# Router logits summed from the old rows' transposed form and eight more columns beside Wo; prefixes among the small moves

## What is computed

```python
x = x + 0.5 * ffn(layernorm(x), ...)
x = x + attn(layernorm(x), ...)        # 16 heads of 8, windows of 64, out @ Wo.T + bo
x = x + 0.5 * ffn(layernorm(x), ...)

# in ffn
r_in = x * rsqrt(mean(x * x) + 1e-6) * rsqrt(d) * router_scale
logits = r_in @ router_w                # 8 experts
top_k_idx = top_k(logits, 2)
out = sum over the two: weight * per_expert_scale * expert(x)
```

## Time and profile before

| | us |
|---|---|
| median of 3 runs | 640.43 |
| lowest, highest | 637.59, 641.42 |
| the profiled execution, device time | 640.15 |
| its span in the trace | 638.1 |
| TensorE busy in the span | 520.2 |
| VectorE, GpSimd, ACT busy | 416.4, 363.3, 277.3 |

### The profile page before, as it was taken

One profiled execution on the slowest core, in us unless ns is written; L12 is line 12 of the kernel. 1 busy time (PEld: TensorE's weight loads), 2 busy tenths in 40 slices (PEclk: granted clock), 3 DMA queues, 4 the chain that ended last, 5 costly groups with the idle time before them and its releaser, 6 DMA issues.

```text
span 638.1 us, 20679 instructions
## 1 busy us (share of the span) xinstructions
PE 520.2 (82%) x7242; PEld 457.1 (72%) x7243; DVE 416.4 (65%) x1431; ACT 277.3 (43%) x627; POOL 363.3 (57%) x425
## 2 busy tenths in 40 slices
PE   0899865999999599999999899999730999999920
PEld 0666635899999478888788778878520999999920
DVE  5776653666676857677688887656324566766747
ACT  0444112443443246666566657555420344434404
POOL 8777775775566431343657565561667556656630
PEclk9999896999999679999899999999855899999975
DMA  9611222222322312010212111120102222323259
GB/s 268 206 48 54 68 70 51 84 71 83 83 82 75 100 51 66 23 52 20 76 30 76 35 40 33 44 55 19 34 27 77 72 81 85 83 74 92 83 143 277
DMA packets 60136, 49.37 MB, mean 77 GB/s; under 512 B 8736, under 2 KB 53536, under 8 KB 59936
## 3 DMA queue, kind: packets, MB, share of 16 engines
q1 hardware_dynamic: 51872, 31.51, 18.6%
q0 software_dynamic: 8192, 16.86, 8.0%
HBM read 23.55 MB, written 20.59 MB: 69 GB/s over the span
## 4 chain that ended last, share of the span: by engine, by line
PE 57%; DVE 13%; POOL 10%; issue 8%; DMA 5%; ACT 3%; SPq 3%; DVEq 0%; POOLq 0%; ACTq 0%
PE PS L560 16%; PE PS L574 7%; PE PS L634 7%; POOL xs_rows L408 6%; PE PS L628 5%; DVE MB L1278 4%; DVE X L1250 4%; PE PS L526 3%; PE PS L549 3%; PE PS L782 2%; POOL ys_rows L423 2%; PE PS L818 2%; DMA XS<-xs_rows 2%; PE PS L624 2%; DMA ys_rows<-YO,XS 1%
## 5 line engine op out<-in xcount | busy, mean ns | idle before, releaser
L423 POOL DMA_INDIRECT ys_rows<-YO,XS x136 | 130.9, 963 | 89.5 <-issue 54.5
L560 PE MATMUL PS<-XST,WG 128*128 128x128 f32 x1088 | 151.3, 283 | 0.0
L408 POOL DMA_INDIRECT xs_rows<-XN,IDX x120 | 118.0, 984 | 36.2 <-issue 34.1
L560 PEld LDWEIGHTS PS<-XST,WG 128*128 128x128 f32 x1088 | 134.9, 195 | 3.9 <-issue 0.2
L1179 DVE TENSOR_TENSOR AV<-PS,GA 128x256 f32<-128x256 f32 x136 | 57.7, 424 | 85.5 <-PE PS L574 43.1
L1278 DVE TENSOR_REDUCE MB<-PS 128x8 f32<-128x1024 f32 x64 | 78.2, 1222 | 42.7 <-PE PS L624 42.4
L893 ACT ACTIVATE GA<-PS 128x256 f32<-128x256 f32 x136 | 52.1, 383 | 95.7 <-PE PS L560 95.5
L574 PE MATMUL PS<-EXP,AV 128*128 x544 | 83.2, 276 | 1.3 <-DVE AV L1179 1.2
L628 PE MATMUL PS<-QM,K 32*128 32x128 f32 x1024 | 76.8, 287 | 5.8 <-DVE MB L1278 4.2
L922 ACT ACTIVATE PT<-PS 128x1024 f32<-128x1024 f32 x64 | 64.4, 1022 | 31.0 <-PE PS L624 17.4
L634 PE MATMUL PS<-MOP,PICKS 32*128 32x128 f32 x1024 | 74.7, 287 | 0.9 <-issue 0.8
(11 more groups left out here) (172 smaller groups left out, 882.0 us busy)
## 6 DMA issues: line engine op xcount, KB each, us to landing
XS<-xs_rows SPq DMA_DIRECT2D x136, 64.5 KB, 1.8
VM<-VM SPq DMA_DIRECT2D x32, 128.0 KB, 2.4
XN<-ys_rows SPq DMA_DIRECT2D x16, 256.0 KB, 5.4
YG<-ys_rows SPq DMA_DIRECT2D x14, 256.0 KB, 2.8
EXP<-experts SPq DMA_DIRECT2D x1, 3072.0 KB, 11.2
ys_rows<-YO,XS POOLq DMA_INDIRECT x136, 2.2
X<-x SPq DMA_DIRECT2D x4, 512.0 KB, 6.3
xs_rows<-XN,IDX POOLq DMA_INDIRECT x120
```

Of the source, the lines that this page charges most:

```text
L408: pool.indirect_dma_start(xs, bass.IndirectOffsetOnAxis(ap=IDX[:, place, c, i:i + 1], axis=0), XN[:, c, place, i, :], None).then_inc(scatt ...
L423: pool.indirect_dma_start(ys, bass.IndirectOffsetOnAxis(ap=XS[:, r, D:D + 1].bitcast(U32), axis=0), YO[:, r, :], None).then_inc(ys_out[r], 16)
L560: ins = pe.matmul(HPS[r % 2][:, c * P:(c + 1) * P], WG[r % 2][:, c * P:(c + 1) * P], XST[r % 2][:, :], start=True, stop=True)
```

## The change

The router's logits are a linear function of `x` but for the scale of each row. They are split: the old rows' part comes from `XAT`, the transposed normalised rows that attention makes anyway, times router weights `RWC` whose column mean is taken off; the attention's part comes from eight more columns beside `WO` (Wo times the router weights), in the same product as the output. `old_sums` multiplies the old part by the row's standard deviation (`SD`) and adds the bias part; the sum of both is `LGX`; `scale_sums` multiplies by `scale` of the new statistics. So the transposes, the copy to `XNT` and the logits of the second router are gone. `old_logits` are two products (four passes) ahead of the small moves of even iterations, for the next sequence.

The prefixes go into `M0` and reach VectorE through the copy to `MOP`, in SBUF. Groups 0 to 3 (`QUICK`) choose experts at 4g+10 and count at 4g+11, groups 4 to 6 at 4g+8 and 4g+9, the last group does both at 4g+8. ACT normalises half of a group at 4g+8 and half at 4g+9 (the last group's all at 4g+8, behind its copy to `MOP`). GpSimd sends groups 0 to 3 one tile an iteration from 4g+12; groups 4 to 6 two tiles at 4g+9 and two at 4g+10; the last group's at i=36. The loop has two iterations less (`TAIL` 5).

Set-up work is put into the first expert phase: at slot 1 TensorE transposes `WO` and `BO` and sums the router weights, at slot 7 it multiplies them, at slot 12 it makes the old logits of the first sequence, with one ACT copy behind each; GpSimd gets one product more in `attention_scales`.

```diff
@@ -272,6 +281,25 @@
             return [n for n, t in enumerate((i, i - 3, i - 4)) if blk(t)]
+        def old_rows(i):
+            return i // TS + 1 if i >= 0 and i % TS == 0 and seq(i // TS + 1) else None
+        def chosen(i):
+            for g in range(GROUPS):
+                if i == g * TG + (8 if g >= QUICK else 10):
+                    return g
+        def counted(i):
+            for g in range(GROUPS):
+                if i == g * TG + (8 if g == GROUPS - 1 else 9 if g >= QUICK else 11):
+                    return g
+        def moves(i):
+            return moved(i) or counted(i) is not None
         block = ctx.enter_context(nc.Block())
...
@@ -458,6 +486,7 @@
...
                 step(pool.tensor_tensor(LN["rstd"][:, :], LN["vareps"][:, :], NHALF[:, 0:TG], ALU.pow))
+                pool.tensor_tensor(SD[:, tiles(g)], LN["vareps"][:, :], LN["rstd"][:, :], ALU.mult)
                 pool.tensor_tensor(LN["shift"][:, :], LN["mean"][:, :], LN["rstd"][:, :], ALU.mult)\
...
@@ -472,6 +501,8 @@
...
                 router_scales(RT, slice(0, TG), PARTS + g)
+                pool.wait_ge(stok_ready, PARTS + g + 1)
+                pool.tensor_tensor(RT["scale"][:, :], RT["rstd"][:, :], RT["stok"][:, :], ALU.mult).then_inc(scale_ready, 1)
                 pool.tensor_tensor(RT["shift"][:, :], RT["mean"][:, :], RT["rstd"][:, :], ALU.mult)\
...
@@ -487,12 +518,18 @@
...
                     scales_of(g)
-                g, part = divmod(i - 11, TG)
-                if 0 <= g < GROUPS - 1:
+                g, part = divmod(i - 12, TG)
+                if 0 <= g < QUICK:
                     if part == 0:
...
                     send_tile(g, part)
-                if group(i, -10) == GROUPS - 1:
+                for lag in (9, 10):
+                    if (g := group(i, -lag)) is not None and QUICK <= g < GROUPS - 1:
+                        if lag == 9:
+                            start_route(len(SENT) + g)
+                        for part in (0, 1) if lag == 9 else (2, 3):
+                            send_tile(g, part)
+                if group(i, -8) == GROUPS - 1:
                     route(len(SENT) + GROUPS - 1, GROUPS - 1)
...
@@ -593,6 +632,19 @@
...
                     step(s // XRING, s % XRING)
+                    if ph == 0 and s == 1:
+                        pe.transpose(SETUP[:, 0:P], WO[:, 0:D], IDN)
+                        pe.transpose(SETUP[:, P:2 * P], BO[:, :], IDN)
+                        pe.matmul(SETUP[:, 2 * P:2 * P + E], ONES, RWS[:, :], start=True, stop=True).then_inc(wr_done, 1)
+                    if ph == 0 and s == 7:
+                        pe.wait_ge(rwc_ready, 1)
+                        for m in range(2):
+                            ins = pe.matmul(SETUP[:, m * E:(m + 1) * E], TURNED[:, m * P:(m + 1) * P], RWC[:, :],
+                                            start=True, stop=True)
+                        ins.then_inc(wr_done, 1)
+                    if ph == 0 and s == 12:
+                        pe.wait_ge(xat_ready, 1)
+                        old_logits(SETUP, 2 * E)
                     if ph == 0 and s in (10, 12, 14):
...
@@ -603,6 +655,11 @@
...
                     step(n // XRING - 1, r)
+            def old_logits(bank, at):
+                for a in range(TS):
+                    pe.matmul(bank[:, at + a * E:at + (a + 1) * E], XAT[:, a * P:(a + 1) * P], RWC[:, :], start=True, stop=True)
             def strip(a):
...
@@ -719,6 +776,8 @@
             def small_moves(i):
+                if old_rows(i) is not None:
+                    old_logits(M0, AT_OLD)
                 for n in moved(i):
...
@@ -727,7 +786,9 @@
...
                         pe.wait_ge(mt_ready, i)
-                        ins = pe.matmul(M0[:, 2 * P:3 * P], MOP[(i - 1) % 2][:, 1, :], WO[:, :], start=True, stop=True)
+                        ins = pe.matmul(M0[:, AT_OUT:AT_OLD], MOP[(i - 1) % 2][:, P:2 * P], WO[:, 0:D + E], start=True, stop=True)
+                if (g := counted(i)) is not None:
+                    ins = prefixes(len(SENT) + g, M0, AT_PX, g == GROUPS - 1)
                 ins.then_inc(mt_done, 1)
...
@@ -736,27 +797,6 @@
...
                 ins.then_inc(to_done, 1)
-            def router_part(i):
-                if any(group(i, -lag) is not None for lag in (8, 9, 10)):
-                    pe.wait_ge(*((pvs_ready, i - 1) if blk(i - 2) else (os_ready, T)))
-                if (g := group(i, -8)) is not None:
-                    pe.wait_ge(px_used, len(SENT) + g)
-                    transposes_of_router(GROUPS + g, g, M1)
-                if (g := group(i, -9)) is not None:
-                    logits(GROUPS + g, M1)
-                if (g := group(i, -10)) is not None:
-                    prefixes(len(SENT) + g, M1, g == GROUPS - 1)
-            def router_part_used(i):
-                if (g := group(i, -8)) is not None:
-                    pe.wait_ge(xnt_ready, GROUPS + g + 1)
-                if (g := group(i, -9)) is not None:
-                    pe.wait_ge(lg_used, GROUPS + g + 1)
-                if (g := group(i, -10)) is not None:
-                    pe.wait_ge(px_used, len(SENT) + g + 1)
             def values(t):
...
@@ -787,25 +827,23 @@
...
                     need(pe, m01_ready, i + 1)
-                if moved(i):
+                if moves(i):
                     small_moves(i)
...
                 round_two(i)
-                router_part(i)
                 round_three(i)
-                if moved(i):
+                if moves(i):
                     pe.wait_ge(mt_ready, i + 1)
...
                 if blk(i - 2):
-                    router_part_used(i)
                     to_tokens(i - 2)
...
             pe.wait_ge(bv_spread, 1)
-            pe.matmul(M1[:, 0:D], BVB[:, :], WO[:, :], start=True, stop=True).then_inc(bvo_done, 1)
+            pe.matmul(M1[:, 0:D], BVB[:, :], WO[:, 0:D], start=True, stop=True).then_inc(bvo_done, 1)
             rows_bank, logits_bank, prefixes_bank = ROUTER
...
@@ -903,10 +942,18 @@
...
                     step(s, s % RING)
+                    if ph == 0 and s == 2:
+                        act.wait_ge(wr_done, 1)
+                        act.copy(TURNED, SETUP[:, 0:2 * P + E]).then_inc(wr_ready, 1)
+                    if ph == 0 and s == 9:
+                        act.wait_ge(wr_done, 2)
+                        act.copy(WO[:, D:D + 2 * E], SETUP[:, 0:2 * E]).then_inc(wr_ready, 1)
                     if ph == 0 and s in (7, 8):
...
                         stage((s - 1) // 2 - 9, EARLY)
+                    if ph == 0 and s == 13:
+                        act.copy(XR, SETUP[:, 2 * E:4 * E]).then_inc(xr_ready, 1)
                 with act.Fori(written // RING, n // RING - 1) as i:
...
@@ -949,26 +996,43 @@
...
                     ins.then_inc(xa_ready, 1)
-            def router_inputs(g):
+            def router_inputs(g, half):
                 act.wait_ge(shift_ready, g + 1)
                 act.wait_ge(scattered, SENDS[0])
-                for a in range(TG):
+                for a in range(half * TG // 2, (half + 1) * TG // 2):
                     normalised(XN[:, 0, g, a, 0:D], g * TG + a, RT, a).then_inc(xn_ready, 1)
             def attend(i):
-                if moved(i):
+                if moves(i):
                     act.wait_ge(mt_done, i + 1)
                     need(act, res_done, i - 5)
-                    parts = slice(moved(i)[0] * P, (moved(i)[-1] + 1) * P)
-                    act.copy(MOP[i % 2][:, :, :].rearrange("p n q -> p (n q)")[:, parts], M0[:, parts]).then_inc(mt_ready, 1)
+                    if i % TS == 0 and i > 0 and seq(i // TS):
+                        act.wait_ge(xr_used, i // TS + 1)
+                    lo = moved(i)[0] * P if moved(i) else AT_PX
+                    hi = (moved(i)[-1] + 1) * P + (E if 2 in moved(i) else 0) if moved(i) else MOVED
+                    if old_rows(i) is not None:
+                        hi = AT_PX
+                    if counted(i) is not None:
+                        hi = MOVED if counted(i) == GROUPS - 1 else AT_SUM
+                    act.copy(MOP[i % 2][:, lo:hi], M0[:, lo:hi]).then_inc(mt_ready, 1)
                 if i == 0:
...
                 if (g := group(i, -8)) is not None:
-                    router_inputs(g)
-                if (g := group(i, -9)) is not None:
+                    router_inputs(g, 0)
+                    if g == GROUPS - 1:
+                        router_inputs(g, 1)
+                        act.wait_ge(xn_ready, TG * (GROUPS + g + 1))
+                        second_rows(g)
+                if (g := group(i, -9)) is not None and g < GROUPS - 1:
+                    router_inputs(g, 1)
+                    if g >= QUICK:
+                        act.wait_ge(xn_ready, TG * (GROUPS + g + 1))
+                        second_rows(g)
+                if (g := group(i, -10)) is not None and g < QUICK:
+                    act.wait_ge(xn_ready, TG * (GROUPS + g + 1))
```

(46 more changed lines are left out.)

## The result

The changed kernel took 641.81 us (median of 12, 638.47 to 643.47) beside 638.91 us of the kernel before on the same chip: ratio 1.0039, 95% interval 1.0022 to 1.0057. On a second chip the same pair gave 641.24 and 640.52 us, 1.0018 [0.9997, 1.0039], and on a third, slower one the ratio was 0.9985 [0.9942, 1.0028]; so the loss is clear of noise on the first chip alone, and a gain is shown on none. I had said 639, a gain of 1.3 us in the profiled execution; its span instead grew by 1.9 us, from 638.1 to 640.0. The time lies inside my range and within 1%, but I had forecast a small gain and it was a small loss.

What follows compares the result with a forecast made beforehand. TensorE was taken to nearly bound the attention loop, a chain of small steps the tail. Loop -0.1, first expert phase +1.2, tail -2.4 gave -1.3 us against 640.15; median forecast 639 us, range 630 to 646.

Steps and rivals of the forecast that it cites:

- i=24: Loop, group 4's choice: scales nearly clear, some 0.5 us cover from masks and maxima; i=24 and 28 together save 1.65 us.
- i=28: Loop, group 5's choice: VectorE waits 3.6 us for GpSimd's late scales, 3.2 reaching TensorE; bounds 0 and 4.2.
- rival 3: Even loop iterations: VectorE sums meeting GpSimd masks at the shared port lose up to 0.97 us each; 639 + 0.97 n; chance 0.15.
- rival 2: Loop, stall at i=28: TensorE's clock falls in one or two more stretches, +1.7 to +3.4 us; chance 0.15.
- The combining iterations: Loop, i=4, 8, 12, 16, 20: VectorE already full, added sums cost +0.4 us each, +2.0 in all.
- Rival 1: Loop and tail: GpSimd is not late and VectorE has room, total -10.7 us, 629.7; chance 0.22.
- The pairs i=2, 3 and i=6, 7: Loop, i=2 and 6: `old_logits` added on TensorE and nothing removed, +1.0 us.
- Iteration 9: Loop, i=9, 13, 17, 21: logits gone, -1.1 us each; copies to `MOP` 6.3 to 6.9 us apart.
- i=25 and 29: Loop: logits out and prefixes in on TensorE, -1.7 us for both.
- The first phase: First expert phase: added set-up transposes, products and copies make it end +1.2 us later; bounds 0.3 and 1.7.
- old logits of i=0: Loop start, i=0: four products stand before maxima that TensorE waits for; iteration +0.7 us, `old_logits` priced at 0.5.
- The tail: Last group's way to its first send: router work gone, but group 6's sends delay its scales; -2.4 us, bounds -6.6 and 0.

Runs made afterwards that it cites:

- masks first: Changed kernel with GpSimd's two sends of iterations 23 and 27 moved behind the query masks of 24 and 28: 634.39 us, 0.9914 of the kernel before.
- with fills: GpSimd's query masks of sequences 2 to 15 replaced by memsets: changed kernel 625.47 us (0.9785), kernel before 637.26 us (0.9953), both relative to the kernel before.
- four edits: Changed kernel with masks before sends, group 6's sends split, last group's ACT rows before the copy, set-up ahead of the first expert phase: 630.66 us, ratio 0.9874.
- single fills: Changed kernel with query masks of sequences 2 to 15 each replaced by one memset, rerun on another chip: 625.89 us, 0.9772 of the kernel before.
- the run with `QUICK` 6: Changed kernel with groups 4 and 5 choosing at 4g+10 and sent one tile an iteration, like groups 0 to 3: 634.56 us, 0.9908 of the kernel before.

## Why the prediction was wrong

**i=24: the step that failed.** "Group 4 also, nearly: its cover is the masks and maxima of i=24". I had counted the masks as cover for the scales. They are the load: VectorE's choice of experts was moved from 4g+10 to 4g+8, right behind the scales, and so into the masks of the same iteration. -0.8 expected, +3.95 found: this one term is off by 4.75 us, more than the whole miss of 3.2 (-1.3 said, +1.9 found). The run with masks first gives 3.7 of it back.

**i=28: the number was right, its cause was not.** +2.4 expected, +2.6 found. GpSimd's scales did start late, at 420.57 us and directly behind a send, as worked out, but 0.9 us behind `vareps` (ready at 419.68) where I had 3.5: counted from the copy of i=25, `vareps` came 1.4 us later and the sends ended 1.2 us earlier than I had them. VectorE came to them late itself and waited 0.61 us, not 3.6. TensorE's 2.93 us came in the main from the masks; the scales alone cost perhaps the 0.9 us that the run with masks first has left there. The sign of it: I had written "VectorE idle on GpSimd's `scale`", and it was busy, on two products for 2.09 us.

**The port, rival 3.** The mechanism was named and given 0.15. Two things were mis-sized. A meeting cost 0.97 us in my rival, the one row I had the earlier trace rows; here it costs 1.8 us (`OH`) plus 0.34 (`IND`), or 0.45 plus 1.7 (`LGX`, `X`), since VectorE stands behind several masks in a row. And I argued that "the sum above carries such meetings as they fall before". The kernel before had 9.0 us of them on VectorE and paid 2.7; the changed one has 14 and pays 15, what the clock loses behind them included. What I took over unchanged was the busy time, and what changed was the slack beside it. The Trainium skill, SBUF — State Buffer, section "Who interferes with whom", which I had weighed against the trace, says that a VectorE instruction with two SBUF inputs contends with a GpSimd instruction that reads SBUF, not with one that only writes it. The 0.28 us of `OH` beside the fills agrees.

**The clock, rival 2** (0.15) came as well, at i=24 and at i=28. It is not independent of rival 3: it follows its waits. A gap of 3 us in TensorE was followed by 4 us at 0.50 and 4 at 0.71, and iteration 24 got 4 us longer from a stop of 2.2.

**The combining iterations: a second step that failed.** I had written that "the transposes that go free nothing" there and that each costs +0.4 us, from i=20 alone. Iterations 4, 8 and 12 got shorter instead, by 0.21, 1.07 and 0.96 us, which I had named as a sign of being wrong; 16 and 20 are 8.00 and 7.88 (+0.46 and -0.06; at least 7.9 said). Together they are -1.8 where +2.0 was said. The reason was wrong even where the number came out: the kernel before takes 7.55 us in 8, 12, 16 and 20 with fills, and the changed one 6.23 or 6.24 in all five, VectorE's added sums included. What makes 16 and 20 long are VectorE's stops. Rival 1, that VectorE has room, is right about the kernel without masks, where the change is worth some 11 us.

**Up to i=24** the loop was 3.8 us shorter where I had said -0.4 and a part of i=0. The combining iterations are 3.8 us of this, and i=13 is 2.5: the kernel before took 10.28 and 10.30 us there (with masks and with fills) and lost the clock in it, the changed one takes 6.70, of which I had forecast -1.1. Against it stand i=17 (+1.8 beside the forecast), i=5 (+0.9) and i=14 (+0.8). The total missed by only 3.2 us although i=24 alone was off by 4.75: that is luck. Chance also has a part in the loop, since which iteration loses the clock differs between profiles. In i=16 TensorE waits 1.80 us in both profiles of the changed kernel; in the first the clock then is 0.50 from 341 to 343 us and i=17 takes 8.10 us, in the second it stays at 1.00 and i=17 takes 6.70.

**Single terms that held.** The pairs i=2, 3 and i=6, 7: +1.0 said, +0.9 found. Iteration 9: 6.3 to 6.9 said, 6.70 found in both profiles, and 6.70 in 13 and 21; in four of the variants 9 takes 7.6 to 8.1.

**Terms that do not follow from their prices.** For i=25 and 29 I had -1.7, but 2 x (-1.1 + 0.5) is -1.2; for i=24 and 28 I had -1.65, but 2 x (-0.66 - 0.47 + 0.5) is -1.3. By the prices that I gave, the sum was some 0.9 us too low.

**The first phase** was +1.2 at the thirteenth slot (122.10 to 123.33) and stays so up to the last in the first profile, +0.5 in the second. The old logits of i=0 then cost 1.02 us and not 0.5, since I priced them at full clock in a stage whose clock I had not looked up; at a clock of 1.00, in i=24, the same four passes take 0.61 us.

**The tail** was right in its parts. Sends of group 6 start 13.05 us behind the copy of i=31 (13.1 said) and the last ends at 23.5 (23.3 said); the first send is at 34.2 (34.4 said, 36.8 before). `vareps` came at 18.0 instead of 19.0, and nothing was gained by it, as the sends held the scales: they start 5.5 us behind it, where I had 4.2.

**The second phase** runs 1.3 us longer, with a granted clock of 0.93 instead of 0.98 in 498 to 520 us. It was not in the sum, and it is not the change: among the profiles at full pace the phase takes 143.1 to 143.5 us or 144.4 to 144.9, and those of masks first (143.12), of four edits (143.48) and of single fills on the second chip (143.28) hold the change and are of the short kind. In the 22 us that start 3 us behind the first slot the clock is 0.97 to 0.99 in the short ones and 0.92 to 0.95 in the long ones.

## What to carry to other kernels

Before work is taken off the engine that bounds, list the stops on the engine beside it that this work was covering: two-input sums of VectorE that fall beside GpSimd's reads count with their stopped length, not with their free one. When a VectorE chain is moved to another iteration, look at what GpSimd does in that iteration; moving two sends behind four masks, in two iterations, was worth 1.0 to 1.2%, more than the whole change cost. A run with fills in place of GpSimd's reads, in both kernels, prices the port in one step. And an iteration's length in the kernel before has to be put down to an engine for each iteration, not for one that stands for all.

## What the runs showed of the hardware

- VectorE's second `OH` product in i=24 takes 1.86 us by itself (the first 0.31) and ends at 395.77 us, behind the third of four masks (2.32 us in all, 0.58 each, from 393.96), and `IND` at 396.34, behind the fourth at 396.28. So a stop of one instruction can last several of GpSimd's in a row. The Trainium skill, SBUF — State Buffer, section "Who interferes with whom", has whoever issues first hold the pair for its whole instruction; the pair in the kernel before would fit one such hold for each product, 1.86 us of a single product do not. The masks get hardly longer: 2.32 us here, 2.33 where they run first, 2.38 beside the sum of `X` in i=16.
- Reductions of maxima out of PSUM did not slow down: 1218 ns mean with masks, 1222 with fills, and 1.21 us in the run with masks first, right beside them.
- Beside one bias sum of GpSimd (1.28 us at 399.92) in the run with `QUICK` 6, an 8-column sum of VectorE took 1.62 us instead of 0.17, though it starts 0.3 us earlier.
- TensorE's clock: behind waits of 2.93 and 3.03 us it fell to 0.50 and was back near 1.00 some 4 to 7 us after TensorE had started again, in both profiles of the changed kernel. Behind shorter waits it goes either way. It stayed at 1.00 behind 0.89 and 1.10 us (masks first); behind 1.80 us it fell in one profile of the changed kernel and not in the other; and in i=13 of the kernel before it fell to 0.50 (315 to 318 us) soon after this short one:

```profile
313.08 0.37 PE L634 MATMUL PS<-MOP,PICKS 32*128 32x128 f32 x1 [0.77 <-issue]
```
